# Decoder layer on one Trainium2 core: the sums of keys times values, added by GpSimd and moved behind the next queries

## What is computed

```
def xattn(q, k, v, Wq, Wk, Wv, Wfc):        # q: normed x; k = v = context
    qp = l2norm(q @ Wq)
    kp = l2norm(k @ Wk)
    vp = v @ Wv
    kv = sum(kp * vp, axis=tokens)          # one vector of 256 per batch
    return (qp * kv) @ Wfc + v
```

## Time and profile before

| What | Value |
|---|---|
| median of 3 runs | 438.69 us |
| profiled execution, span | 435.8 us |
| TensorE busy | 410.3 us (94%) |
| VectorE busy | 341.1 us (78%) |
| ScalarE busy | 310.6 us (71%) |
| GpSimd busy | 237.4 us (54%) |
| mean granted TensorE clock | 0.990 |

### The profile page before, as it was taken

One profiled execution on the slowest core, in us unless ns is written; L12 is line 12 of the kernel. 1 busy time (PEld: TensorE's weight loads), 2 busy tenths in 40 slices (PEclk: granted clock), 3 DMA queues, 4 the chain that ended last, 5 costly groups with the idle time before them and its releaser, 6 DMA issues.

```text
span 435.8 us, 8737 instructions
## 1 busy us (share of the span) xinstructions
PE 410.3 (94%) x2921; PEld 382.3 (88%) x2921; DVE 341.1 (78%) x828; ACT 310.6 (71%) x623; POOL 237.4 (54%) x350
## 2 busy tenths in 40 slices
PE   7888999999999998999999999999999999999970
PEld 6676888889888887989999999999999999999970
DVE  4646757776867989986777798979999899979950
ACT  3835576676756575757569988889889889889720
POOL 4614546666655658588754455544656356543431
PEclk9999999999999999999999999999999999999995
DMA  8911020202110160884499697996999879895631
GB/s 275 345 26 50 2 74 25 74 26 75 49 50 25 40 241 26 299 304 166 113 280 362 161 326 226 316 325 208 377 282 298 282 253 316 298 347 126 191 36 12
DMA packets 32464, 79.60 MB, mean 183 GB/s; under 512 B 4674, under 2 KB 23746, under 8 KB 26532
## 3 DMA queue, kind: packets, MB, share of 16 engines
q1 hardware_dynamic: 23456, 67.94, 43.9%
q0 software_dynamic: 7488, 10.39, 12.0%
q10 hardware_dynamic: 1476, 0.72, 0.6%
HBM read 69.40 MB, written 9.63 MB: 181 GB/s over the span
## 4 chain that ended last, share of the span: by engine, by line
PE 75%; DVE 9%; POOL 5%; issue 3%; ACT 3%; DMA 2%; ACTq 0%; SPq 0%; POOLq 0%; DVEq 0%
PE bank L424 57%; PE bank L431 4%; PE bank L862 3%; PE bank L701 2%; PE bank L660 2%; PE bank L721 1%; PE bank L843 1%; PE bank L667 1%; DMA aw_f<-aw_ 1%; PE bank L642 1%; DVE ohB L1391 1%; POOL cT_l L2048 1%; DMA y_<-yb,idxs 1%; DVE st L1325 1%; DVE w1l L1449 1%
## 5 line engine op out<-in xcount | busy, mean ns | idle before, releaser
L2087 POOL DMA_INDIRECT y_<-yb,idxs x29 | 55.5, 1913 | 75.9 <-DMA y_<-yb,idxs 45.5
L424 PE MATMUL bank<-xh,w1h 128*128 128x256 f32 x256 | 74.8, 292 | 0.7 <-issue 0.7
L424 PE MATMUL bank<-w2h,hh 128*128 128x256 f32 x264 | 75.3, 285 | 0.0
L424 PE MATMUL bank<-w2l,hh 128*128 128x256 f32 x264 | 74.1, 281 | 0.0
L424 PE MATMUL bank<-w2h,hl 128*128 128x256 f32 x264 | 74.1, 280 | 0.0
L424 PE MATMUL bank<-xh,w1l 128*128 128x256 f32 x256 | 72.4, 283 | 0.0
L424 PE MATMUL bank<-xl,w1h 128*128 128x256 f32 x256 | 72.3, 283 | 0.0
L1449 DVE TENSOR_TENSOR w1l<-w1r,w1h 128x1024 fp32r<-128x1024 f32 x46 | 56.0, 1220 | 0.9 <-ACT w1h L969 0.6
L2027 POOL DMA_INDIRECT xg<-xn_rows,idxg x39 | 46.0, 1180 | 14.0 <-issue 10.8
L424 PEld LDWEIGHTS bank<-w2h,hh 128*128 128x128 f32 x264 | 50.0, 189 | 0.0
L424 PEld LDWEIGHTS bank<-w2l,hh 128*128 128x128 f32 x264 | 50.0, 189 | 0.0
(11 more groups left out here) (258 smaller groups left out, 1083.2 us busy)
## 6 DMA issues: line engine op xcount, KB each, us to landing
w1r<-ff_ SPq DMA_DIRECT2D x23, 1024.0 KB
w2r<-ff_ SPq DMA_DIRECT2D x23, 1024.0 KB
b1r<-b_ SPq DMA_DIRECT2D x7, 512.0 KB
bs<-ff_ SPq DMA_DIRECT2D x23, 132.0 KB
xn_rows<-xn SPq DMA_DIRECT2D x8, 264.0 KB, 2.5
xin<-x_ SPq DMA_DIRECT2D x8, 256.0 KB, 6.7
cT<-ctxT_ SPq DMA_DIRECT2D x8, 256.0 KB, 5.1
cin<-ctx_ SPq DMA_DIRECT2D x8, 256.0 KB, 3.5
```

The costliest lines, as they stand in the source:

```text
L424: r = e.matmul(o, a_(t), b_(t), start=first and m == 0, stop=m == n - 1)
L2087: e.indirect_dma_start(out=out[:, :], out_offset=bass.IndirectOffsetOnAxis(ap=at, axis=0), in_=yb[t % 2][:, i, :], in_offset=None, compute ...
```

## The change

GpSimd gets a new last step in each stage, `summed(s)`: it adds the second half of `wkv` to the first, in place. TensorE's four products with ones go from the end of `attention(s)` to the start of `projected(s)`, a stage later and behind the next queries (behind `count` and `xpose(0)` for the last batch), and become two, over the added half, into bank 3 in place of bank 2. `projected` no longer waits for `a_kvc`. On ScalarE the copy of the sums and the scalings into `fcs` leave `attended` and become `sums(b)`, behind `exp_q(s)` and before `context_high(s)`; for the last batch behind `x_affine(0)`.

```diff
 def attention(s):  # tensor
...
-                for m in range(2):
-                    for i in range(2):
-                        last = e.matmul(banks[2][:, m:m + 1], wkv[n][:, i, m * 128:(m + 1) * 128],
-                                        const("ones")[:, 0:1], start=i == 0, stop=i == 1)
-                last.then_inc(p_kvc, 1)
 def projected(b):  # tensor
...
+                e.wait_ge(g_ws, b + 1)
+                for m in range(2):
+                    last = e.matmul(banks[3][:, m:m + 1], wkv[k][:, 0, m * 128:(m + 1) * 128],
+                                    const("ones")[:, 0:1], start=True, stop=True)
+                last.then_inc(p_kvc, 1)
                 e.wait_ge(a_aT, b + 1)
-                e.wait_ge(a_kvc, b + 1)
...
 def attended(b):  # scalar
...
                 e.activation(aT[k][:, :, :], banks[0][:, :], ACT.Copy).then_inc(a_aT, 1)
+
+            def sums(b):
+                k = b % 2
                 e.wait_ge(p_kvc, b + 1)
-                e.activation(kvc[:, k, :], banks[2][:, 0:2], ACT.Copy).then_inc(a_kvc, 1)
+                e.activation(kvc[:, k, :], banks[3][:, 0:2], ACT.Copy).then_inc(a_kvc, 1)
...
 loop of scalar
                 if s != 1:
                     exp_q(s)
                 if s >= 1:
+                    sums(s - 1)
                     context_high(s)
...
             x_affine(0)
+            sums(NB - 1)
             x_high(0)
...
 gpsimd
+            def summed(s):
+                w = wkv[s % 2]
+                e.wait_ge(v_wkv, 2 * s + 2)
+                e.tensor_tensor(w[:, 0, :], w[:, 0, :], w[:, 1, :], ALU.add).then_inc(g_ws, 1)
...
                 if s >= 1:
                     scale_q(s - 1)
+                summed(s)
```

More of the change, by code:

```diff
@@ L321, in decoder_layer @@
             sem(f"v_{n}") for n in ("x2Tl", "wkv", "qml", "x2", "xn", "inv", "cnt"))
-        g_va, g_rs, g_cTl, g_xc, g_rb, g_rm = (sem(f"g_{n}") for n in ("va", "rs", "cTl", "xc", "rb", "rm"))
+        g_va, g_rs, g_cTl, g_xc, g_rb, g_rm, g_ws = (sem(f"g_{n}") for n in ("va", "rs", "cTl", "xc", "rb", "rm", "ws"))
         r_v, r_p, r_w, r_g, r_h, r_x, r_e, r_ex, r_cnt, r_invT, r_sel = (
```

## The result

The changed kernel takes 447.26 us (median of 4 runs, 444.17 to 450.38), the kernel before 438.32 in the same measurement: ratio 1.0158, interval 1.0097 to 1.0219. The ratio isn't the quotient of the medians (1.0204): it and its interval are estimated from the executions in the faster of two states that the kernel has. The kernel is slower, by 1.6% as the best estimate and by 1.0% at the lower end of the interval; the forecast had given "slower by over 1%" 0.43 and "within 1%" 0.54. The forecast of 443.0 us, a ratio of 443.0 / 438.69 = 1.0098, was too low, and the median lies 1.1 us above the end of its range. The profiled execution took 448.12 us with a span of 446.2.

A forecast was written before the change was run, and what follows sets the result against it. TensorE sets the pace in stage 4, with late chains through other engines in stages 5 to 7; 2.61 + 1.59 - 0.23 + 0.33 = +4.30 us, on the median 438.69 giving 443.0 us (1.0% more), range 440.2 to 446.2.

The forecast's parts named there:

- TensorE was full: Rival: at stage boundaries transposes follow TensorE's queue, so removed products give time back; 2.7 us less, 436.0; 5 in 100.
- the add catches the reciprocal: Rival: GpSimd's addition holds VectorE's reciprocal some 0.5 us in seven boundaries; 3.5 us more, 446.5; 10 in 100.
- Steps 1 and 5: Stage boundary: removing 0.82 us of products gains 0 in stages 2 to 7; GpSimd's 0.74 us addition costs nothing there.
- Step 2: Behind the next queries: two products, four passes, put 0.41 us on the path of the projection and everything behind it.
- Step 3: ScalarE's sums behind the exponents: products with fcs start 0.87 us later, 0.46 of it new wait, overlapping the moved products.
- Step 4: context_high behind the sums: cT_l, and GpSimd's queue behind it, 0.53 us later; stages 5 to 7 grow 0.53 each.
- signs that I had named for being wrong: Stages at 19.85 us or below, no wait before fcs products, reciprocals over 0.25 us, late-stage growth clearly off 0.53.
- The third rival: Late stages swallow more: stages 5 to 7 cost 0.36, 0.02, 0.14, the end nothing; 2.9 us, 441.6; 20 in 100.
- Step 6: First and last stages: stage 1 gains 0.23 us; behind the loop later xc holds xn, +0.33, between 0 and 0.7.
- Moved as a whole: Feed-forward part behind the loop: it waits for the loop's results and only shifts with them; 435.8 us span becomes 440.1.
- the second rival of the forecast: GpSimd's addition holds VectorE's reciprocal some 0.5 us in seven boundaries; 3.5 us more, 446.5; 10 in 100.

The follow-up runs named there:

- e6: Kernel before plus GpSimd's addition in each stage, its result written where nobody reads it: loop 121.08 us, tail 8.05 us; one execution, no ratio.
- e2: Kernel before with ScalarE's new order alone, the four products in their old place but into bank 3, no addition: loop 125.13 us, ratio 1.0064.
- e3: Changed kernel without GpSimd's addition, four products behind the queries in place of two: 0.13 us more in the loop, tail 7.01 us; no ratio.
- e4: Changed kernel with context_high ahead of the exponents: loop 124.87 us, +4.3 us in the medians against the kernel before.
- e11: Kernel before with one wait on GpSimd, xc in stages 3 to 6 only after VectorE's four ohB masks: loop 119.70 us, interval up to 1.0008.
- e12: Kernel before, xc waiting for the masks in stages 3 to 6, in stage 7 behind first gather and masks: 436.82 us against 440.01, ratio 0.9941.
- e5: Changed kernel with the two products between the transposes of at_s and the queries, ScalarE's order of before, addition kept: loop 121.46 us.

## Why the prediction was right, and where it was not

**Direction: right; mechanism: right for the largest term, wrong for the late stages and for what follows the loop.** Of the rivals, "TensorE was full" falls by the 0.83 us of idle time ahead of the transposes, and "the add catches the reciprocal" by the reciprocals, 0.25 us as before, also where the addition came first.

**Steps 1 and 5: right.** Nothing was gained at the boundary; the addition measures 0.73 us (taken: 0.74) and costs the loop nothing (e6).

**Step 2: 0.36 us for four passes, taken 0.41.** It doesn't matter, since the wait behind it takes up the difference: without moved products the start is the same (e2), and with eight passes it is 0.05 us later (e3).

**Step 3, the largest term: right.** Predicted +0.87 for the start of the products with `fcs`, found +0.84; the new wait was to be 0.46 of it and is 0.41 by the starts, though the row itself shows 0.24 of idle time. Stage 4 grew by 0.96: 0.84, and 0.10 since the products behind a wait last 1.99 us and not 1.89. Stages 2 to 4 were to grow by 2.61 and grew by 2.93 (0.89, 1.08, 0.96). Against the second trace of before the figure for stage 3 is 0.6 only (20.91 - 20.32), since `xc` meets the masks there.

**Step 4: sum near, mechanism wrong.** The +1.59 for stages 5 to 7 came out as +0.53, +0.21, +0.52 = +1.26; stage 6, clearly below 0.53, was one of the signs that I had named for being wrong. I gave each the delay of `cT_l`, 0.53. e4 took that delay away and +1.04 stayed. What counts is the rule I had as the smaller of two: TensorE's own new length, less the old wait. With the 0.96 of stage 4 and old excesses of 0.51, 0.94 and 0.64 us over 19.85 (the forecast had 0.85 and 0.73 from the stretches cut at 146.20) it gives 0.45, 0.02 and 0.32, together 0.79, against 1.04 in e4. The third rival described this, though it priced it too low with 0.36, 0.02 and 0.14. And the old waits were not GpSimd's queue as such, but `xc` holding VectorE's masks and `x2l` (e11, e12). In the changed kernel that hold costs next to nothing: with masks of 1.99 us stages 3 and 6 last 20.91 and 21.00 us in its first trace, with masks of 1.00 us 20.80 and 20.98 in its second.

**Step 6: place and mechanism right, size just over the upper bound.** +0.33 was taken between 0 and 0.7; the tail grew by 0.73 in the first traces and 0.77 in the second, and e6 shows that the addition alone does it. I had `xn` held for a part of `xc`; it was held for all of it. The first `xn` starts 60 ns ahead of `xc` and ends at 178.04 + 1.48 = 179.52, 0.15 us behind the end of `xc` at 178.10 + 1.27 = 179.37, and the second comes after it. Stage 1 gained 0.13, not 0.23.

**The sum.** Loop +4.19, tail +0.73, stage 1 -0.13: +4.79 us against 4.30. By the second traces it is 3.61 + 0.77 - 0.15 = 4.23. That 4.30 lies between them is in part luck: step 4 was 0.33 too high for a wrong reason, steps 3 and 6 were 0.32 and 0.40 too low.

**What the forecast didn't have, and what stays open.** The two spans differ by 10.4 us; the medians by 8.9 here and by 6.4 in the second measurement (447.39 against 440.99), the ratios by 6.9 us (interval 4.3 to 9.6) and 6.2 us (3.4 to 8.9). Of the 10.4, 4.8 are the sum above. Another 1.1 us lie ahead of stage 1, and the second traces have them the other way round (30.30 before, 29.11 after). They are the clock's and not the change's: up to there the granted clock is 0.94 in the traces that take 30.3 us and 1.00 in those that take 29.1. The rest, 1.0 us in the expert tiles and 3.5 at the end, is there in both pairs of traces, with a granted clock of 1.00 in the expert tiles. "Moved as a whole", the last step of the forecast, failed there. The 1.0 us are a wait near the end of the tiles. VectorE's `yb` waits for the landing of an earlier scatter, the low part `hl` behind it is late (it ends at 424.84 + 1.28 = 426.12), and TensorE stands still until then; the traces of the kernel before have no such gap there:

```profile
423.44 0.35 DVE L1764 TENSOR_SCALAR yb<-ya,small 128x256 f32<-128x256 f32 x1 [1.41 <-DMA y_<-yb,idxs]
...
426.23 0.35 PE L424 MATMUL bank<-w2h,hh 128*128 128x256 f32 x1 [0.96 <-issue]
```

The end has few lengths, and what they are is in GpSimd's scatters, which run one behind the landing of another. First after, then e4, whose loop is nearly the same:

```profile
429.32 1.54 POOL L2097 DMA_INDIRECT y_<-yb,idxs  x1 [2.98 <-DMA y_<-yb,idxs]
...
435.65 1.54 POOL L2097 DMA_INDIRECT y_<-yb,idxs  x1 [2.95 <-DMA y_<-yb,idxs]
```

```profile
428.33 1.54 POOL L2100 DMA_INDIRECT y_<-yb,idxs  x1 [1.43 <-DVE yb L1767]
432.76 1.54 POOL L2100 DMA_INDIRECT y_<-yb,idxs  x1 [2.88 <-DMA y_<-yb,idxs]
```

In e4 the scatter before the last waits for its data only; after, a backlog of one landing is left (429.32 waits for a DMA), and the chain that ended last runs through these scatters for 20% of the span (1% in the kernel before, 3% in e4):

```profile
PE bank L424 28%; DMA y_<-yb,idxs 20%; POOL y_ L2097 4%; DVE w1l L1453 3%; PE bank L431 3%; PE bank L861 3%; PE bank L671 3%; DVE w2l L1712 2%; PE bank L705 2%; PE bank L642 1%; DVE at_s L1579 1%; ACT tq L1038 1%; DVE hl L1741 1%; DMA aw_f<-aw_ 1%; PE bank L594 1%
```

Whether such a backlog arises is not tied to the loop: e12 has the shortest loop and an end of 16.9, e4 a long loop and 13.1. What starts it was not settled, so it stays open how much of the 6 to 9 us belongs to the change beyond the 4.2 to 4.8 shown. Both intervals include 4.4 us, so the times alone don't rule out that it is nothing, though both pairs of traces have the 4.5 us. e2, e4 and e5 come out at +3.6, +4.3 and +1.6 us in the medians (+2.8, +4.5 and +0.7 by the ratios), and their loop and tail (against the second trace of before) at +3.5, +4.2 and +0.9. The kernel before itself, measured against itself, came out at +1.3 in the medians, so these agreements are no closer than about a microsecond.

## What to carry to other kernels

Before moving work off a busy engine, look at what released the instruction behind it: here four of eight passes were saved in time that TensorE spent waiting for VectorE, and the move put `kvc` and `fcs` behind 1.5 us of exponents in ScalarE's order. An engine that works in order makes a moved instruction late by everything it is now queued behind, and that alone was the price in the loop (e2); the addition cost 0.7 to 0.9 us behind it (e3, e6). And where two engines hold each other, the start of the longer instruction is worth an explicit wait: `xc` begun 0.5 us too early (12.12 us into stage 5 in place of 12.63 in e11) cost 0.5 us of a stage in which TensorE was busy for 20.08 of 20.36 us.

## What the runs showed of the hardware

A GpSimd instruction can hold VectorE's, and VectorE's can hold GpSimd's. `x2l` takes 0.41 us and up to 1.38 beside `xc` or `cT_l`; the two `xn` 1.81 in place of 0.93; the four fp16 masks 1.98 in place of 1.00; GpSimd's square root 1.24 in place of 0.71 beside `ohA`. A held instruction of VectorE ends 0.15 us (`x2l`, `xn`) or 0.05 us (a mask) behind the end of GpSimd's. Reciprocals of 16 columns (0.25 us) and `at_s` (0.42 us), which reads a bank, were not held in any trace, although they ran beside the 0.73 us addition at nearly every boundary.

The Trainium skill, "SBUF — State Buffer", section "Who interferes with whom", lists a `tensor_scalar` among the operations that can take the pair of ports shared with GpSimd, the second to start being blocked until the first ends. All three held kinds of VectorE are `TENSOR_SCALAR`, and the durations agree with being blocked until GpSimd ends. Who comes first does not follow from the starts in the profile: the first `xn` starts 60 ns ahead of `xc`, by its row, and is the one that is held, while `xc` keeps its 1.27 us. For `ohA` and the square root it does: a lead of 16 to 26 ns of `ohA` holds GpSimd's instruction for 0.5 us, and a lead of 43 to 48 ns of the square root holds neither (0.71 and 0.69 us). Reciprocals are not named in that section's list, and the runs bear it out: the second rival of the forecast had no ground.

Eight passes of 256 columns behind a wait of TensorE took 1.99 us and the same eight without one 1.89 to 1.95. And a trace of the same kernel may differ by 0.5 us in one stage, because `xc` starts 0.6 us into the masks or 0.2 us behind them, which hangs on two starts that lie within 50 ns of each other: two traces of before are worth having when a change is sized by a single one.
